# Perceiver layers on one core: late projections of the first self attention moved into its loop's block, and late units of the second expert layer held until sorted rows have landed

## The reference, cut to what matters

```python
x = x + _L0_xattn_ref(_layernorm(x), ctx_1024, ...)     # one head
x = x + _L0_attn_ref(_layernorm(x), ...)                # first self attention
x = x + _L0_ffn_ref(_layernorm(x), ...)                 # 16 experts, 4 of them per token, one shared
x = x + _L1_xattn_ref(_layernorm(x), ctx_1024, ...)     # 16 heads
x = x + _L1_attn_ref(_layernorm(x), ...)                # second self attention, projections of rank 64
x = x + _L1_ffn_ref(_layernorm(x), ...)                 # second expert layer: 8 experts, 2 per token
```

```python
qkv = einsum("bnd,ed->bne", xn, w_qkv)                  # w_qkv is 3072 x 512, 16 heads of 64
sim = einsum("bhid,bhjd->bhij", q * 64 ** -0.5, k)
sim = where(causal, mask_value, sim)                    # within a sequence of 32 rows
out = einsum("bhij,bhjd->bhid", softmax(sim), v)
y = einsum("bne,de->bnd", out, w_out) + b_out
```

```python
scores = x @ gate_w.T                                   # 8 experts
topk_scores, topk_idx = top_k(scores, 2); probs = softmax(topk_scores)
h12 = einsum("btd,ehd->bteh", x, w12); hidden = silu(h12[..., :1024]) * h12[..., 1024:]
y = sum over the chosen experts of probs * (hidden @ w3[e].T)
```

## Time and profile before

| | |
|---|---|
| time, median of 3 runs | 2026.59 us (2024.24 to 2028.37) |
| the profiled execution's own time | 2029.76 us |
| its span (first to last instruction) | 2028.0 us |
| instructions | 38297 |
| PE busy | 1755.0 us, 87% |
| DVE, ACT, POOL busy | 887.2, 613.1, 821.7 us |
| DMA | 254.01 MB, mean 125 GB/s |

### The profile page before, as it was taken

One profiled execution on the slowest core, in us unless ns is written; L12 is line 12 of the kernel. 1 busy time (PEld: TensorE's weight loads), 2 busy tenths in 40 slices (PEclk: granted clock), 3 DMA queues, 4 the chain that ended last, 5 costly groups with the idle time before them and its releaser, 6 DMA issues. The chain is left out here.

```text
span 2028.0 us, 38297 instructions
## 1 busy us (share of the span) xinstructions
PE 1755.0 (87%) x13882; PEld 1411.0 (70%) x13882; DVE 887.2 (44%) x1766; ACT 613.1 (30%) x1229; POOL 821.7 (41%) x542
## 2 busy tenths in 40 slices
PE   6785999883899997899999999968983698999999
PEld 5443777662687785788888888856762486878777
DVE  4446262447557854222333333333656433333332
ACT  3112151441233334233333333334653211111111
POOL 1001342113548985233333323313114199794922
PEclk8996999986899998999999999975996799999999
DMA  6582001853657797111111111022304455452534
GB/s 232 213 339 81 29 1 63 303 221 137 228 173 235 245 221 202 32 33 34 41 31 31 39 34 31 12 79 99 141 1 162 170 170 179 145 185 97 172 68 99
DMA packets 108934, 254.01 MB, mean 125 GB/s; under 512 B 9712, under 2 KB 26736, under 8 KB 108816
## 3 DMA queue, kind: packets, MB, share of 16 engines
q1 hardware_dynamic: 77472, 189.86, 27.4%
q0 software_dynamic: 10752, 25.34, 5.4%
q10 hardware_dynamic: 20592, 37.22, 5.4%
HBM read 182.24 MB, written 70.13 MB: 124 GB/s over the span
## 5 line engine op out<-in xcount | busy, mean ns | idle before, releaser
L140 PE MATMUL banks<-ra_DE 128*128 128x258 f32 (+2 forms) x912 | 321.0, 353 | 28.0 <-ACT fa_DE L2435 8.5
L141 PE MATMUL banks<-ra_DE 128*128 128x258 f32 (+2 forms) x912 | 310.8, 342 | 0.0
L142 PE MATMUL banks<-ra_DE 128*128 128x258 f32 (+2 forms) x912 | 310.0, 341 | 0.0
L140 PE MATMUL banks<-weights_F,rest_r_F 128*128 x552 | 229.7, 416 | 14.8 <-ACTq L1953 12.2
L140 PEld LDWEIGHTS banks<-ra_DE 128*128 128x128 f32 (+1 forms) x912 | 177.1, 195 | 61.4 <-ACT fa_DE L2435 15.0
L142 PE MATMUL banks<-weights_F,rest_r_F 128*128 x552 | 218.5, 396 | 0.0
L141 PE MATMUL banks<-weights_F,rest_r_F 128*128 x552 | 218.2, 395 | 0.0
L142 PEld LDWEIGHTS banks<-ra_DE 128*128 128x128 f32 (+1 forms) x912 | 177.8, 195 | 19.2
L141 PEld LDWEIGHTS banks<-ra_DE 128*128 128x128 f32 (+1 forms) x912 | 178.3, 196 | 16.1
L1900 POOL TENSOR_TENSOR weights_F<-rest_F,weights_F 128x1536 fp32r<-128x1536 f32 x52 | 182.0, 3501 | 4.2
L2402 POOL TENSOR_TENSOR fa_DE<-fa_DE 128x1028 f32<-128x1028 f32 x32 | 60.9, 1902 | 254.5 <-DVE fa_DE L2498 254.5
(11 more groups left out here) (491 smaller groups left out, 3507.9 us busy)
## 6 DMA issues: line engine op xcount, KB each, us to landing
rest_F<-in_L_units SPq DMA_DIRECT2D x52, 768.0 KB, 4.3
rest_C<-in_L_units SPq DMA_DIRECT2D x28, 768.0 KB, 4.8
fa_DE<-in_ctxT SPq DMA_DIRECT2D x32, 514.0 KB, 3.9
e_sorted<-zeros_AB SPq DMA_DIRECT2D x1, 12220.0 KB, 36.8
rest_C<-e_sorted ACTq DMA_DIRECT2D x47, 260.0 KB
e_y_scratch<-zeros_AB SPq DMA_DIRECT2D x1, 12032.0 KB, 67.7
e_y_scratch<-rest_C ACTq DMA_DIRECT2D x47, 256.0 KB, 5.0
tail_F<-in_L_units SPq DMA_DIRECT2D x12, 768.0 KB, 21.5
```

The source lines that it names most:

```text
L140: pe.matmul(psum, lh, rh, start=first, stop=False)
L141: pe.matmul(psum, lh, rl, start=False, stop=False)
L142: return pe.matmul(psum, ll, rh, start=False, stop=last)
```

## The change

In the first self attention (`low_rank` false) the first block keeps the eight jobs of token half 0. The eight of token half 1 become `later`, the keys' ones first; they go into the loop's block: TensorE runs one after `scores(1, 1)`, then `values(0, 0)`, then the other seven, using banks 7, 4, 3 in turn, and VectorE copies them out between and after its two first `turned`. ScalarE's `qk_tile` waits for all eight copies from the fourth tile on, and so does `values` of TensorE from the second on. ScalarE's split of half 2's query weights waits for all eight products. POOL's second `x_tile` waits for the first four of them, because its target now lies where the key weights are; the first `x_tile`'s target lies behind the query weights. In the second expert layer SP waits, ahead of unit 8, until the first tile of sorted rows has landed. The second self attention takes the other branch of each condition and `both_halves`, which is not touched.

```diff
--- before.py
+++ after.py
@@ -940,8 +940,35 @@
             wqk = wq
             s_w = programs[3] if hh == 0 else programs[0][3] + programs[1][3]
             s_mm, s_out = sem(f"{name}_qk_product"), sem(f"{name}_qk_taken")
-            jobs = [(k, e, h) for k in range(2) for e in range(EC) for h in range(NHALF)]
+            if low_rank:
+                jobs, later = [(k, e, h) for k in range(2) for e in range(EC) for h in range(NHALF)], []
+            else:
+                jobs, later = [(k, e, 0) for k in range(2) for e in range(EC)], [(k, e, 1) for k in (1, 0) for e in range(EC)]
             NB = 4
+            LATER_BANKS = (7, 4, 3)
+
+            def take(job, bank):
+                k, e, h = job
+                dst = (qt, kt)[k][:, e, h * HALF:(h + 1) * HALF]
+                if low_rank:
+                    b = (bqc, bkc)[k][:, hh * EC + e:hh * EC + e + 1]
+                    ins = dve.tensor_scalar(dst, banks[:, bank, :], b, None, ALU.add)
+                else:
+                    ins = dve.tensor_copy(dst, banks[:, bank, :])
+                ins.then_inc(s_out, 1)
+
+            def project(job, bank):
+                k, e, h = job
+                cols, tok = slice(e * P, (e + 1) * P), slice(h * HALF, (h + 1) * HALF)
+                if low_rank:
+                    rows = slice(DH * k, DH * k + DH)
+                    ins = mm3(banks[:, bank, :], wqk[0][rows, cols], wqk[1][rows, cols], rqk[0][rows, tok], rqk[1][rows, tok])
+                else:
+                    w = (wq, wk)[k]
+                    for c in range(DC):
+                        ins = mm3(banks[:, bank, :], w[0][:, c, cols], w[1][:, c, cols], xh[:, c, tok], xl[:, c, tok],
+                                  c == 0, c == DC - 1)
+                ins.then_inc(s_mm, 1)
 
             with nc.Block() as block:
                 rest = ((2,) if low_rank else (1, 2, 3)) if hh == 0 else None
@@ -972,40 +999,28 @@
 
                 @block.vector
                 def _(eng):
-                    for j, (k, e, h) in enumerate(jobs):
+                    for j, job in enumerate(jobs):
                         eng.wait_ge(s_mm, j + 1)
-                        dst = (qt, kt)[k][:, e, h * HALF:(h + 1) * HALF]
-                        if low_rank:
-                            b = (bqc, bkc)[k][:, hh * EC + e:hh * EC + e + 1]
-                            ins = dve.tensor_scalar(dst, banks[:, j % NB, :], b, None, ALU.add)
-                        else:
-                            ins = dve.tensor_copy(dst, banks[:, j % NB, :])
-                        ins.then_inc(s_out, 1)
+                        take(job, j % NB)
 
                 @block.tensor
                 def _(eng):
-                    for j, (k, e, h) in enumerate(jobs):
+                    for j, job in enumerate(jobs):
                         if j >= NB:
                             eng.wait_ge(s_out, j - NB + 1)
-                        cols, tok = slice(e * P, (e + 1) * P), slice(h * HALF, (h + 1) * HALF)
-                        eng.wait_ge(s_w[0 if low_rank else k], 1)
-                        if low_rank:
-                            rows = slice(DH * k, DH * k + DH)
-                            ins = mm3(banks[:, j % NB, :], wqk[0][rows, cols], wqk[1][rows, cols],
-                                      rqk[0][rows, tok], rqk[1][rows, tok])
-                        else:
-                            w = (wq, wk)[k]
-                            for c in range(DC):
-                                ins = mm3(banks[:, j % NB, :], w[0][:, c, cols], w[1][:, c, cols], xh[:, c, tok],
-                                          xl[:, c, tok], c == 0, c == DC - 1)
-                        ins.then_inc(s_mm, 1)
+                        eng.wait_ge(s_w[0 if low_rank else job[0]], 1)
+                        project(job, j % NB)
 
 
             f, r = Area(fa, F_SIZE, f2), Area(ra, R_SIZE, r2)
             qg, kg, vg = ([f.take(EC, P) for _ in range(2)] for _ in range(3))
             sh, ex, pt = ([f.take(HH, NQ) for _ in range(2)] for _ in range(3))
             mx, sums, rinv = (f.take(2, HH) for _ in range(3))
-            xg = [(r.take(P), r.take(P)) if low_rank else (r.take(DC, P), r.take(DC, P)) for _ in range(2)]
+            if low_rank:
+                xg = [(r.take(P), r.take(P)) for _ in range(2)]
+            else:
+                past = Area(ra, R_SIZE, r2 + 4 * DC * HD)
+                xg = [(a.take(DC, P), a.take(DC, P)) for a in (past, r)]
             ot = [(r.take(EC, P), r.take(EC, P)) for _ in range(2)]
             (s_g, s_v, s_vg, s_s, s_sh, s_ex, s_pb, s_o, s_oh, s_ol, s_y, s_xa, s_links) = (
                 sem(f"{name}_{n}") for n in ("tile", "v", "v_kept", "scores", "shifted", "exp", "p_turned", "o",
@@ -1058,6 +1073,8 @@
                             pool.tensor_tensor(x[:, n, :], x[:, n, :], bo, ALU.add).then_inc(s_xb, 1)
 
                     x_tile(0, 0)
+                    if later:
+                        eng.wait_ge(s_mm, len(jobs) + EC)
                     x_tile(1, 1)
                     if hh == 0:
                         following[0][2](eng)
@@ -1069,6 +1086,8 @@
                 def _(eng):
                     def qk_tile(n, u):
 
+                        if later and not (isinstance(n, int) and n < 3):
+                            eng.wait_ge(s_out, len(jobs + later))
                         eng.wait_ge(s_s, n + 1)
                         act.activation(qg[u], qt[:, :, bass.ts(n, P)], ACT.Copy)
                         act.activation(kg[u], kt[:, :, bass.ts(n, P)], ACT.Copy).then_inc(s_qk, 1)
@@ -1114,6 +1133,8 @@
                     keep_v(0, 0)
                     qk_tile(2, 0)
                     if hh == 0:
+                        if later:
+                            eng.wait_ge(s_mm, len(jobs + later))
                         following[0][1](eng)
                     all_steps(act, step)
 
@@ -1176,7 +1197,14 @@
                     links.enter(0, 2 * STEPS)
                     for n in range(2):
                         shifted(n, n)
+                    for n in range(2):
                         turned(n, n)
+                        if later:
+                            eng.wait_ge(s_mm, len(jobs) + n + 1)
+                            take(later[n], LATER_BANKS[n])
+                    for j in range(2, len(later)):
+                        eng.wait_ge(s_mm, len(jobs) + j + 1)
+                        take(later[j], LATER_BANKS[j % 3])
                     links.leave(1)
                     all_steps(dve, step, lambda i: links.enter(i, 2 * STEPS), lambda: links.leave(NT // 2 - 2))
 
@@ -1201,6 +1229,8 @@
 
                     def values(n, u):
                         eng.wait_ge(s_g, n + 1)
+                        if later and not (isinstance(n, int) and n == 0):
+                            eng.wait_ge(s_out, len(jobs + later))
 
                         eng.wait_ge(s_xa, n + 1)
                         if low_rank:
@@ -1239,7 +1269,16 @@
 
                     scores(0, 0)
                     scores(1, 1)
-                    values(0, 0)
+                    for j, job in enumerate(later):
+                        if j == 1:
+                            values(0, 0)
+                        if j >= 3:
+                            eng.wait_ge(s_out, len(jobs) + j - 2)
+                        project(job, LATER_BANKS[j % 3])
+                    if later:
+                        eng.wait_ge(s_out, len(jobs + later) - 2)
+                    else:
+                        values(0, 0)
                     all_steps(pe, step)
 
 
@@ -1859,6 +1898,9 @@
                             eng.wait_ge(s_split, n - STAGED + 1)
                         elif n >= R and n - R < plan.preloaded:
                             eng.wait_ge(s_split, n - R + 1)
+                        if not plan.shared and n == U:
+
+                            eng.wait_ge(s_rows[0], 16)
                         plan.load_unit(eng, w, n, e if r < E else E)
                     if to is not None:
                         s_out = sem("x_stored")
```

## The result

The changed kernel took 2014.62 us (median of 4 runs, 2011.05 to 2016.3) where the kernel before took 2027.02 on the same chip (4 runs, 2024.24 to 2028.37). The ratio is 0.9932, with a 95% interval of 0.9911 to 0.9953: 13.8 us less (the interval allows 9.5 to 18); forecast were 14.8 less and 2011.8. The profiled execution of after took 2011.05, the fastest of its four, with a span of 2009.3; that of before took 2029.76, more than any of its four. So the two traces lie further apart than the medians.

A forecast was written before the change was run, and what follows sets the result against it. TensorE was taken to bound the attention loop, the first sorted rows' landing the second expert layer's start. Gains of 4.6 (half 1), 4.9 (half 2) and 5.3 (rows) make 14.8 us: 2026.6 to 2011.8, range 2006.5 to 2019.5.

The forecast's parts named there:

- it only ends sooner: Half 2: SyncE's zero fill for the expert tables starts some 21 us earlier with the loop's block, at no cost.
- half 2's 4.9 us: Half 2's gain: 4.52 us idle plus 1.32 at the first step, less a 0.9 us stall for key weights.
- 6.6 us for 4.6: Half 1's forecast gain, 4.6 us: 3.56 idle plus 2.58 at the first step, less a new 1.5 us stall.
- The idle 3.56 us and the first step's 2.58: Half 1: TensorE's wait before the first step goes, and that step falls from 9.96 to 7.38 us.
- the stall: Half 1, before the second step's values: a new 1.5 us wait for the first output's addition, bounds 0 and 3.
- scatter 2.0 us for 1.8: Second expert layer: scatter alone after the eighth unit gains 1.8 us; bounds 0 (keeps 160 bytes a ns) and 2.3 (421).
- load of the rows 3.9 for 3.5: First sorted rows' load takes 3.0 us, the median of 23 such loads, for 6.51: 3.5 gained, between 2.5 and 4.
- the shares of 62 to 38: Unit loads and scatter at 261 and 160 bytes a ns; equal turns left open, by which the hold would give 5.8 us.
- The clock did not fall at the stall: Rival, chance 0.20: clock falls at half 1's new 1.5 us stall, costing 2 us; 2013.8 us.
- the rows come no earlier: Rival, chance 0.10: scatter keeps its rate and the rows' load is slow by itself; hold gains 0, 2017.1 us.
- the softmax ring sets the pace: Rival, chance 0.10: ScalarE and VectorE, not TensorE, pace the loop; moved projections gain 0, 2021.3 us.
- The held units were not late: Rival, chance 0.05: held units land 27.7 us after issue, ScalarE stands 16.4 us; 2028.2 us, or 2031.2.

The follow-up runs named there:

- fill_later: Changed kernel, with half 2's zero fill begun only when the second moved product is done; 2012.26 us, ratio 0.9919 to the kernel before.
- before_fill_later: Kernel before, with half 2's zero fill begun only when the first tile's values are made; half 2 takes 120.53 us, for 120.86 in before.
- b_only: Kernel before, with only SyncE's hold of the unit loads added, no moved projections; 2022.71 us, ratio 0.9981.
- queries_first: Changed kernel, with moved products of queries ahead of keys' and the split of half 2's query weights earlier; 2010.72 us, ratio 0.9915 to the kernel before.
- a_only: Kernel before, with only the moved projections, no hold of the unit loads; 2019.31 us, ratio 0.9963.
- fill_in_half_one: Changed kernel, with the zero fill issued in half 1's loop block in place of half 2's; one execution took 2005.45 us.
- all_three: Changed kernel, with fill after the second moved product, hold ahead of unit 6, and queries first among moved products; 2002.70 us, ratio 0.9876 to the kernel before.
- hold_six: Changed kernel, with the hold ahead of unit 6 in place of unit 8; 2012.48 us, ratio 0.9921 to the kernel before.

## Why the prediction was right, and which step was not

**The time.** 13.8 us for 14.8. That it came so close is in part luck. The touched pieces of the two traces show 13.1 us, but 2.0 us more in half 1 and 0.7 more in the rows stand against 4.4 less in half 2; by the means of all traces it is 11.3 us: 1.0 more in half 1, 0.2 more in the rows and 4.7 less in half 2. The rest of the 13.8 is within what the measurement cannot tell.

**The step that failed** is the sentence "it only ends sooner" on the zero fill, and with it half 2's 4.9 us. I had counted TensorE as needing no DMA there. It does need one, for its own instructions. The cover that this load had, 4.52 us of idle time, is exactly what the change removes. By steps half 2 gave 21.2 us in the first block (as forecast, 21.5) and 1.3 at the first step (1.32); the stretch between the first scores and that step took 4.0 us more than the sum had it, 3.98 of it the stand. That its cause is the fill is shown by `fill_later`, and by the seven traces with moved products: all four with the fill at the block's start have the stand, all three without it do not. That the cost was hidden before is shown by `before_fill_later` beside `b_only`.

**Half 1** gave 6.6 us for 4.6. The idle 3.56 us and the first step's 2.58 went as worked out, the stall was 1.36 us for 1.5, with `queries_first` for its cause. The missing 2 us are in the clock. In the kernel before nine matrix instructions of 0.63 us follow the first scores, at the lower level of 1.2 GHz; in after it is three, before they take 0.40: 1.3 us. At the first block's start eleven ran at the lower level, and six in after: 0.9 us; there the idle time had not brought the lower level about, as the granted clock was 0.50 long before (from 180 to 198 us in before, from 176 to 195 in after). Of these 2.2 us about half is the accident of two executions, the clock's, which I had put into the range only: half 1 is 119.42 to 120.26 us long without the moved products, 113.68 to 115.71 with them, 5.6 us apart in the mean. The rest may belong to the change. After the first scores ten, eight and eight instructions of 512 columns took 0.55 us or more in the three traces without the moved products, and four to six in six of the seven with them (eight in `fill_later`). No run settles that.

**The rows.** The forecast held with its terms: scatter 2.0 us for 1.8, load of the rows 3.9 for 3.5, as it took 2.58 us, less than the median I used. The scatter alone reached 373 bytes a ns, near the 421 of the upper bound and far from 160. The Trainium skill (DMA: Bandwidth & Descriptors, section Queues, rings and completion order) has each engine go round its queues a packet at a time; the trace agrees, as the lone queue inherits most of the rate. The prediction said that the shares of 62 to 38 leave an equal turn open; the earlier trace rows had the answer, which I overlooked: 1059 packets on either queue, so the turns were equal and the packets were not (5.4 and 3.3 KB). Behind the rows something may have been given back at first: 1572 to 1577 runs at clock 0.50, and POOL's first split comes 33.85 us after the rows for 32.37. But the longest wait behind the rows, which the trace ends with ScalarE's signal and which that in turn gives when POOL's split is done, is no sign of it. It is 5.70 us for 3.89 before, yet 5.42 in `before_fill_later`, which holds nothing. The piece as a whole was no longer.

**The rivals.** The clock did not fall at the stall: it lasted 1.36 us, less than the 1.42 of the earlier trace rows, and the products after it took 0.39 us. The row that spoke for this rival was misread. The product after 1.93 us of idle was slow because the clock was low already, not through that gap; stretch of the kernel before:

```profile
1327.00:1333.00 6.00, 3.48 (x74) 3.08 (x74) 1.36 (x4) 1.23 (x2) 1.11 (x2) 0.50 0.00 0
```

That the rows come no earlier, or that the softmax ring sets the pace (40.00 of 40 us busy), is refuted by the rows above; `b_only` and `a_only` show each part gaining alone. The held units were not late. What did happen was on no list: a cost that the removed idle time had hidden.

**Open** are why the late load costs nothing in half 1; why, if the queues take turns, the instruction packet is seen 3.4 us later under the fill at all; how much of half 1's surplus belongs to the change; and all that lies below the 2 to 5 us by which untouched stages vary.

## What to carry to other kernels

Idle time that is to be filled may be hiding other waits; ask of each engine what it also fetches there, its own instructions included. In this kernel a large fill that nobody waits for did better behind the first products of a block than at its start: some 4 us in half 2, though nothing in half 1 or before the change. And transfers wanted last should not run beside the small, scattered ones that the next stage waits for.

## What the runs showed of the hardware that was not expected

- A load of TensorE's instructions, 16 KB in one packet, is late when the DMA engines are full. With no fill it was in the trace 0.9 to 1.1 us after the first scores of half 2 (`fill_later`, `fill_in_half_one`, `all_three`, `before_fill_later`); with 24 MB of zeros under way at 383 GB/s it was there 4.5 or 4.6 us after them, and TensorE stood 3.98, 3.14, 2.96 and 3.04 us in four kernels (after, `a_only`, `hold_six`, `queries_first`), each time until 2.4 us after the packet's start. The profile calls this idle time "issue" and gives it no releaser; the queue of kind "instruction" shows it.
- Unit loads and scatter on two queues moved equal numbers of packets (1059 and 1059 before, 778 and 772 after) and so shared the rate by the packets' sizes, 261 and 160 bytes a ns; alone the scatter reached 373.
- After equal idle times of 2.47 us, and with the same code in half 1, four matrix instructions of 512 columns took 0.55 us or more in one execution (after) and eight in another (`fill_later`); together with a longer slow stretch at the first block's start (six and fourteen instructions) half 1 took 113.68 and 115.71 us.
